# Dense attention's diagonal maxima: masked in SBUF by GpSimd instead of by products on TensorE

## The reference, cut to what matters

```
q, k, v = split(heads(x @ W1 + b1), 3)
w = einsum('bhqd,bhkd->bhqk', q, k) / dk
w = w * mask - 1e10 * (1 - mask)          # mask = lower triangle
w = softmax(w, axis=-1)
attn = einsum('bhqk,bhkd->bhqd', w, v)
out = attn @ W2 + b2
```

## Time and profile before

| what | us |
|---|---|
| median of three runs | 3261.07 (3250.24 to 3267.6) |
| the profiled execution | 3263.65 |
| its span, first to last instruction | 3261.9 |
| dense attention's rounds, in that span | 1666.8 to about 2985 |
| TensorE busy (share of the span) | 2705.5 (83%) |
| VectorE busy | 1716.2 (53%) |
| ScalarE busy | 1459.0 (45%) |
| GpSimd busy | 871.4 (27%) |
| VectorE's reductions of the dense maxima (L1379) | 680.4 in 576 |
| ScalarE's exps of the dense scores (L1421) | 583.0 in 576 |

### The profile page before, as it was taken

The page is one execution under the profiler, slowest core; times in us unless marked ns, Lnnn a source line. Parts: engine busy times, 40 slices in busy tenths (PEclk is TensorE's granted clock), DMA queues, the critical chain, the costliest instruction groups (busy, mean ns, idle before and its releaser), DMA issues. The chain is left out here.

```text
span 3261.9 us, 102182 instructions
## 1 busy us (share of the span) xinstructions
PE 2705.5 (83%) x46240; PEld 1572.6 (48%) x46240; DVE 1716.2 (53%) x2797; ACT 1459.0 (45%) x1537; POOL 871.4 (27%) x561
## 2 busy tenths in 40 slices
PE   2688888988888886698579899998989898997897
PEld 1456565655655565443334444444444444443443
DVE  3356445454445544610666666666666666664501
ACT  1344444454544443421235554555555554555522
POOL 3343434353434432000412122222222121211002
PEclk8788898989888987899779999999999999999998
DMA  8333324343333331489042122222222122220498
GB/s 203 79 94 82 99 67 101 81 115 79 93 83 84 91 91 38 122 342 380 26 91 59 42 59 59 60 60 59 60 60 59 43 59 48 60 51 7 184 419 325
DMA packets 232618, 343.72 MB, mean 105 GB/s; under 512 B 113396, under 2 KB 141240, under 8 KB 215800
## 3 DMA queue, kind: packets, MB, share of 16 engines
q1 hardware_dynamic: 206952, 309.35, 33.0%
q10 hardware_dynamic: 25232, 27.83, 3.6%
HBM read 266.02 MB, written 68.71 MB: 103 GB/s over the span
## 5 line engine op out<-in xcount | busy, mean ns | idle before, releaser
L1379 DVE TENSOR_REDUCE b_tops<-b_slot 128x8 f32<-128x1024 f32 x576 | 680.4, 1220 | 336.7 <-PE b_slot L1228 173.5
L1421 ACT ACTIVATE b_probs<-b_slot 128x1024 f32<-128x1024 f32 x576 | 583.0, 1023 | 526.6 <-PE b_slot L1236 372.3
L1178 POOL TENSOR_SCALAR_AFFINE_SELECT b_probs<-b_probs 128x1024 f32<-128x1024 f32 x128 | 139.8, 1093 | 728.6 <-ACT b_probs L1421 728.6
L519 POOL COPY a_q_far<-a_q_near 96x1024 bf16<-96x1024 bf16 x128 | 259.7, 2058 | 254.4 <-PE a_slot L596 193.2
L1256 PE MATMUL b_outT_ps<-b_probs,b_v 128*17 128x128 f32 (+3 forms) x4608 | 319.2, 385 | 6.2 <-ACT b_probs L1421 5.5
L1236 PE MATMUL b_slot<-b_q_stack,b_k_stack 99*128 99x512 bf16 (+3 forms) x1280 | 274.8, 321 | 42.8 <-DVE b_tops L1379 32.1
L905 ACT ACTIVATE a_k_far<-a_k_near 96x1024 bf16<-96x1024 bf16 x128 | 257.8, 2063 | 90.5 <-DMA a_k_near<-parts_near_dram 82.1
L1236 PE MATMUL b_slot<-b_k_stack,b_q_stack 96*128 96x512 bf16 (+3 forms) x1280 | 266.7, 323 | 30.9 <-DVE b_tops L1379 20.7
L799 DVE TENSOR_TENSOR a_probs<-a_slot,a_bias_k 128x1024 f32<-128x1024 f32 x128 | 154.7, 1218 | 135.1 <-PE a_slot L596 134.9
L868 ACT ACTIVATE a_probs<-a_probs 128x1024 f32<-128x1024 f32 x128 | 133.1, 1051 | 176.0 <-DVE a_probs L799 175.9
L808 DVE TENSOR_REDUCE a_tops<-a_slot 128x16 f32<-128x1024 f32 x128 | 156.0, 1220 | 104.0 <-PE a_slot L596 103.0
(11 more groups left out here) (227 smaller groups left out, 4325.6 us busy)
## 6 DMA issues: line engine op xcount, KB each, us to landing
f_w_ring<-in_L_ffn_w_dram SPq DMA_DIRECT2D x128, 1024.0 KB, 17.7
parts_near_dram<-a_parts ACTq DMA_DIRECT2D x96, 256.0 KB
parts_dram<-b_parts SPq DMA_DIRECT2D x96, 256.0 KB
a_k_near<-parts_near_dram SPq DMA_DIRECT2D x128, 128.0 KB, 2.9
b_k_stack<-parts_dram SPq DMA_DIRECT2D x64, 256.0 KB, 7.0
a_q_near<-parts_near_dram SPq DMA_DIRECT2D x64, 192.0 KB, 2.9
b_q_stack<-parts_dram SPq DMA_DIRECT2D x32, 384.0 KB, 4.5
values_dram<-a_v_stage SPq DMA_DIRECT2D x16, 544.0 KB
```

The lines of the kernel that those rows point to most:

```text
L519: pool.tensor_copy(q_far[far][0:QK_ROWS, h, :].rearrange("p (r a) -> p r a", r=LINKS), q_near[near][0:QK_ROWS, h, :].rearrange("p (a r) -> ...
L1178: pool.affine_select(out=blocks, in_=blocks, compare_op=ALU.is_ge, fill=0.0, base=0, pattern=[[0, NT], [1, P]], channel_multiplier=-1).the ...
L1379: ins = dve.tensor_reduce(out, src, AX.X, ALU.max)
L1421: act.activation(probs_of(b, g, u, h)[:, :], slot_of(step)[:, :], ACT.Exp).then_inc(taken_act, 1)
```

## The change

The diagonal units of the maxima become steps `md`. TensorE computes their eight blocks without the two mask products. ScalarE copies the slot to a new SBUF tile `diagonal` (128x1024, one buffer), GpSimd puts the very negative number above the diagonal there with an `affine_select`, and a new step `mdr` lets VectorE reduce `diagonal` into `tops`. So the slot of such a unit is now given back by ScalarE. ScalarE's copy waits for the reduction of the diagonal unit before (`diagonal_reduced`), VectorE's reduction for the select (`diagonal_masked`), and `mred` also for the last of them. `maxima` now takes the units of u = 1 to 4 in their order and puts a diagonal unit in at the places 0, 4, 8 and 12 of the 18, and each `mdr` two beats after its `md`. The constant `v_wide`, used in the layer before, moves to that layer's own memory.

```diff
         units = beat_units("mx", b, g)
-        for n, step in enumerate(units):
-            out[n * (BEATS - 5) // len(units)].append(step)
+        beside = units[HG:]
+        for h in range(HG):
+            beside.insert(4 * h, ("md", b, g, 0, h))
+        for n, step in enumerate(beside):
+            beat = n * (BEATS - 5) // len(units)
+            out[beat].append(step)
+            if step[0] == "md":
+                out[beat + 2].append(("mdr",) + step[1:])
...
-    BY_ACT = ("S", "zt", "v", "at")
+    BY_ACT = ("S", "zt", "v", "at", "md")
...
+        diagonal = sb("diagonal", [P, N])
...
+                    elif step[0] == "md":
+                        pool.wait_ge(taken_act, count("taken_act", *step))
+                        blocks = diagonal[:, :].rearrange("p (j k) -> p j k", k=P)
+                        pool.affine_select(out=blocks, in_=blocks, compare_op=ALU.is_ge, fill=NEG, base=0,
+                                           pattern=[[0, NT], [-1, P]], channel_multiplier=1).then_inc(diagonal_masked, 1)
...
                         if u == 0:
-                            for c in range(2 if kind == "mx" else 0):
-                                pe.matmul(dst[:, 512 * c:512 * (c + 1)], ident16[:, :], later[:, :].unsqueeze(1).to_broadcast([P, 4, P]),
-                                          start=True, stop=False, skip_group_check=True)
                             for tile in range(NT):
                                 mine = slice(P * tile, P * tile + P)
-                                ins = pe.matmul(dst[:, mine], own[0:rows, h, mine], other[0:rows, h, mine], start=kind == "S", stop=True,
-                                                skip_group_check=True)
+                                ins = pe.matmul(dst[:, mine], own[0:rows, h, mine], other[0:rows, h, mine], start=True, stop=True)
...
                         dve.wait_ge(taken_dve, count("taken_dve", "mx", b, g, UNITS - 1, HG // 2 - 1))
+                        dve.wait_ge(diagonal_reduced, count("mdr", "mdr", b, g, 0, HG - 1))
...
+                    elif kind == "mdr":
+                        _, b, g, u, h = step
+                        if h == 0 and (prev := before(b, g)):
+                            dve.wait_ge(mred_done, count("mred", "mred", *prev))
+                        dve.wait_ge(diagonal_masked, count("mdr", *step))
+                        dve.tensor_reduce(tops[:, h, 0:NT], diagonal[:, :].rearrange("p (c k) -> p c k", k=P), AX.X, ALU.max).then_inc(diagonal_reduced, 1)
...
+                    elif kind == "md":
+                        act.wait_ge(filled, nth["filled", step])
+                        hold(act, diagonal_reduced, count("md", *step) - 1)
+                        act.activation(diagonal[:, :], slot_of(step)[:, :], ACT.Copy).then_inc(taken_act, 1)
```

More of the change, by code:

```diff
@@ L1044, in dense_constants @@
     return {"wqk": sb("wqk", [P, 2, KD, H, HD]), "wv": sb("wv", [P, KD, H, HD]), "wout": sb("wout", [P, KD, D]), "bqk": sb("bqk", [P, 2, 2]),
-            "v_bias": sb("v_bias", [P, KD]), "v_wide": sb("v_wide", [P, KD, P]), "o_bias": sb("o_bias", [P, D]),
+            "v_bias": sb("v_bias", [P, KD]), "o_bias": sb("o_bias", [P, D]),
             "ident16": sb("ident16", [P, P], BF16), "later": sb("later", [P, P], BF16)}
@@ L1051, in dense_attention @@
     BY_DVE = ("mx", "q", "k", "ot", "op", "mt")
-    BY_ACT = ("S", "zt", "v", "at")
+    BY_ACT = ("S", "zt", "v", "at", "md")
     nth, total = {}, {}
     for name, kinds in {"filled": BY_DVE + BY_ACT, "taken_dve": BY_DVE, "taken_act": BY_ACT, "qk": ("q", "k"), **{kind: (kind,) for kind in (
-            "S", "PV", "ote", "z", "mred", "part0", "rest1", "part1", "part2", "mrow", "xb")}}.items():
+            "S", "PV", "ote", "z", "mred", "part0", "rest1", "part1", "part2", "mrow", "xb", "md", "mdr")}}.items():
         for step in seq:
@@ L1117, in dense_attention @@
             sem(n) for n in ("part0_done", "rest1_done", "part1_done", "part2_done", "mrows_in"))
+        diagonal_masked, diagonal_reduced = sem("diagonal_masked"), sem("diagonal_reduced")
         spilled = [sem(f"spilled{n}") for n in range(2)]
@@ L1209, in _ @@
                     kind = step[0]
-                    if step[:3] == ("mx", 0, 0) and step[3:] == (0, 0):
+                    if step == ("md", 0, 0, 0, 0):
                         pe.wait_ge(cleared, N_CLEARED)
-                    if kind in ("S", "mx"):
+                    if kind in ("S", "mx", "md"):
                         _, b, g, u, h = step
@@ L1374, in _ @@
                             _, b, g, u, h = step
-                            if u == 0 and h == 0 and (prev := before(b, g)):
-                                dve.wait_ge(mred_done, count("mred", "mred", *prev))
                             out = tops[:, h, NT * u:NT * u + NT] if u < 4 else tops[:, 2 * h:2 * h + 2, 4 * NT:4 * NT + NT // 2]
@@ L1572, in ffn @@
                 dense, wd = beside
+                v_wide = ssb("v_wide", [P, KD, P])
                 n_loads = 3 * KD + 3 * 2 + 2
@@ L1661, in _ @@
                         for kd in range(KD):
-                            ins = pe.matmul(bank[3][:, 0:D], dense["v_wide"][:, kd, :], dense["wout"][:, kd, :], start=kd == 0, stop=kd == KD - 1)
+                            ins = pe.matmul(bank[3][:, 0:D], v_wide[:, kd, :], dense["wout"][:, kd, :], start=kd == 0, stop=kd == KD - 1)
                         ins.then_inc(through_out, 1)
@@ L1775, in _ @@
                         for kd in range(KD):
-                            dve.tensor_copy(dense["v_wide"][:, kd, :], dense["v_bias"][:, kd:kd + 1].to_broadcast([P, P])).then_inc(wide_ready, 1)
+                            dve.tensor_copy(v_wide[:, kd, :], dense["v_bias"][:, kd:kd + 1].to_broadcast([P, P])).then_inc(wide_ready, 1)
                         dve.wait_ge(through_out, 1)
```

## The result

The changed kernel takes 3337.65 us (median of four runs, 3328.59 to 3345.46) against 3264.34 of the kernel before beside it: a ratio of 1.0226, 95% interval 1.0191 to 1.0261. It is slower, as forecast, but by 73 us and not by 27, and outside the range.

The account below looks back on a forecast made before the run. Rounds were taken as bound by TensorE and the slot ring behind VectorE's reductions in turns. 14 x 1.4 + 6 x 1.0 - 7 x 0.4 + 4 x 1.2 - 1.0 = +26.6 us on 3261 gave 3288, range 3238 to 3312.

Parts of the forecast that it names:

- The walk: Unit-by-unit timing of round 2.1 through TensorE, the slots and VectorE's queue; claimed +1.4 us per group 1 round.
- `q` at 13.1: Group 1 round: the `q` projection starts 13.1 us after the first score unit, as before the change.
- S(2,1) at 23.4: Second half of round 2.1: this score unit starts at 2070.21 instead of 2069.08, 1.13 us later.
- the tie to the ring: Three PSUM slots used in turn by all TensorE work except PV; S(2,1) gets the fourth reduction's slot, 1.13 us later.
- `k` at 30.1: Group 1 round: the `k` projection starts 30.1 us after the first score unit instead of 28.7.
- the round of 43.0 us: Group 1 rounds of dense attention take 43.0 us instead of 41.6.
- Group 2: Rounds with the `v` projection: the second `v` starts 0.4 us earlier, -0.4 us a round.
- group 0: Rounds with the output projection: S(2,0) waits for mx(2,3) behind the third `diagonal` reduction, +1.0 us a round.
- The reduction from SBUF: VectorE's four reductions of `diagonal` per round, taken at 1.14 us each, the pace from PSUM.
- short-reduction rival: VectorE's reduction from SBUF takes only 0.75 us: 3261 to 3265, no change; 0.19 together with a swallowed shift.
- ScalarE and GpSimd: Copies of 1.02 us and selects of 1.09 us, 4.1 and 4.4 us a round, beside TensorE's products, costed at nothing.
- the last rival: TensorE drops to 1.2 GHz behind the new waits, 1.7 us in each of 24 rounds, 41 us more: 3329; chance 0.09.

Follow-up runs that it names:

- e3: Changed kernel with the two mask products put back ahead of the second and fourth diagonal unit of a round, their result overwritten; 3303.65 us, 1.0141 to before.
- e6: Changed kernel with VectorE's reductions of the masked copies moved later in its queue, and four bf16 `diagonal` buffers; 3232.81 us, 0.9903 to before.
- e4: Changed kernel with VectorE's maximum of the masked copy taken over its first 8 columns alone, copies and selects kept; 3210.58 us, 0.9860 to before.
- e9: Changed kernel with four bf16 buffers for the masked copies, reductions at the changed kernel's places; 3344.62 us, 1.0228 to before.
- e1: Kernel before without its two mask products per diagonal unit, mask left out, reductions still reading PSUM; 3224.27 us, 0.9901 to before.
- e7: Changed kernel with the two mask products put back ahead of the first and third diagonal unit of a round; 3349.12 us, 1.0248 to before.
- e8: Kernel before without mask products and with diagonal units at the changed kernel's places, no copies or selects; 3229.53 us, 0.9893 to before.

## Why the prediction was wrong

- *The walk* held. `q` at 13.1, S(2,1) at 23.4 and the tie to the ring are in after's rows; `k` at 30.1 and the round of 43.0 us are in e3's, where the clock stays up. Group 2 came out 0.3 to 0.5 us shorter in its five rounds at clock 1.00 (forecast 0.4). In group 0 the two rounds of after without half clock, 3.0 and 6.0, take 47.60 us, 1.23 more than before's one such round, 5.0 (46.37); I had 1.0.
- *The reduction from SBUF* at 1.14 us: 1.12 from start to start. The Trainium skill's "VectorE: DVE Perf Modes" (The perf-mode tier table) has one mode only for it, and the trace agrees, in bf16 too (2.34 for two in e6). The short-reduction rival is out for this kernel; e4, with a reduction of 151 ns, shows that it named the quantity that decides.
- *ScalarE and GpSimd* at nothing: e4 and e6, in which they do all their work, agree. The wait of the second copy for `diagonal`, put at 0.4 us, was 0.5 (in e6, without it, the copy starts at +5.86, in after at +6.36); e9, without it too, is 3 us shorter in the rounds.
- *"Gain: nothing"* in the first half is what came, but not because the products were worth nothing there. Without the detour they gain 1.1 us a round (e1), and the two reductions of `diagonal` ahead of mx(1,3) and mx(2,0) use that up (`q` starts at +13.08 in after, and at +11.67 in e6, which has them behind it).
- *The step that failed* is the last rival. "TensorE's clock falls in the new waits" was set at 0.09 and as a case apart, priced at 41 us *more*. It was a term of the forecast's own sum, and stood there at nothing: the same walk that forecast the waits had to ask what the clock does behind them. Of the 74 us in the rounds, the walk's terms for these 31 rounds make 27.6. The 46 that are left come with 153 us more at half clock, and single rounds give a like price: 44.30 with 3.4 us at half clock (round 2.1 of after) against 43.03 without (e3), 1.3 us. I had taken 1.7 a stretch and, at the worst, one stretch in each of 24 rounds. There are 153 / 3.4 = 45 more stretches, at 46 / 45 = 1.0 us each on the average.
- *What stays open*: not all of the 153 us stand behind new waits. In group 0 the wait for `zb` of 1.81 us is in both kernels. Behind it the six rounds have 24 us at half clock before (3.4 us in four, 10.2 in one, none in one) and 41 us after (10.2 in four, none in two). No run here shows why these 17 us came.
- *Why I had put it at 0.09*: the waits of 0.45 and 0.52 us in round 2.1 before had left the clock at 1.00. But the walk had given waits of 1.4 and 0.7 us in the same place, and the only row with a wait of TensorE over a microsecond, 1.81, did have the clock at 0.50 behind it, as in five of the six rounds of group 0. The nearest row by place was taken where the nearest by length was wanted. Behind the new waits of 1.19 and 1.21 us the clock fell in most rounds of after and e7 (the last section counts them). The rule of the Trainium skill's "TensorE: Matmul & The Clock Gate" (A second HAM failure mode: psum-queue depth-cycling), that short idling between groups of products while PSUM is cycled can make the clock swing, agrees with this.
- With one stretch in each of the 24 rounds, at 1.3 to 1.7 us, the sum would have been 3319 to 3329 and the range's upper end 3303 + 41 = 3344. That range holds the result, but the sum is still 9 to 19 us low, because there are 45 stretches and not 24.

## What to carry to other kernels

Where a walk forecasts new waits on TensorE, price the granted clock behind them in the same sum, by the waits in the trace that come nearest in length and what the clock did behind them. Look at every round that has the wait: the same wait can do both. Work that is moved to another engine is judged by where it stands in that engine's queue: here four reductions a round cost 109 us ahead of those that hold slots (after against e8) and nothing behind them (e6 against e8). And idle time on the engine that paces a stretch, with TensorE as releaser, says that TensorE's work lies on the path there, even where TensorE waits elsewhere.

## What the runs showed of the hardware

- More work on TensorE made the kernel faster: 64 pairs of products in its waits took 123 us off the half-clock time and 29 us off the rounds (e3 against after).
- Waits of the same length did not always do the same to the clock. Behind the 1.19 us before mx(1,3) it fell in ten of the fourteen rounds of groups 1 and 3 of after (in round 2.3 from 7.8 us into it) and not in the other four, among them 2.1. Behind the 1.21 us before the fourth diagonal unit it fell in all fourteen of after and of e7, and in five of fourteen in e3, where products stand behind it in place of the wait of 0.51 us. Behind the 1.81 us for `zb` it fell in five of six rounds of before. What decides stays open.
- A reduction of 8 columns takes 151 ns, one of 1024 takes 1209, in fp32 (e4, after) and in bf16 alike (e6).
